# Routed tokens placed in a fixed area per expert, scattered batch by batch, with zeros written behind each expert's last token

## The chip, the cores and the metric

The kernel runs on one core of one Trainium2 chip. The core has a matrix engine (PE), a vector engine (DVE), a scalar engine (ACT), a general engine (POOL, also called GpSimd) and a queue engine (SP) that mostly issues DMAs. Each of them runs its own list of instructions in order, and they wait for one another only through semaphores. The metric is the time of one execution on the device in microseconds (us); lower is better.

## The reference

Two transformer decoder layers, width 128, on x of 4 batches x 512 tokens:

```python
x = x + L0_attn(layernorm(x))            # causal, 16 heads of 8
x = x + L0_xattn(layernorm(x), ctx)      # 77 context tokens
x = x + L0_ffn(layernorm(x))             # 8 experts, top 2
x = x + L1_attn(layernorm(x))
x = x + L1_xattn(layernorm(x), ctx)
x = x + L1_ffn(layernorm(x))             # ternary weights, conv over tokens
```

The change lies in L0_ffn:

```python
gate_logits = jnp.einsum('bsd,de->bse', x, gate_w) + gate_b
weights, indices = jax.lax.top_k(gate_logits, TOP_K)        # 2 of 8
weights = jax.nn.softmax(weights, axis=-1)
h = jnp.einsum('bsd,edh->ebsh', x, w1) + b1[:, None, None, :]
xh, gh = jnp.split(h, 2, axis=-1)
act = jax.nn.silu(gh) * xh                                  # 512 wide
out_e = jnp.einsum('ebsf,efd->ebsd', act, w2) + b2[:, None, None, :]
sel = jnp.take_along_axis(out_e, indices[..., None], axis=2)
return jnp.sum(sel * weights[..., None], axis=2)
```

## The kernel before

All 2048 tokens stay in SBUF as 16 tiles (NT) of 128 tokens, four per batch (QT = 4, NB = 4). The first stream of work is 32 attention units, numbered g: 0 to 15 for the causal self-attention (A0), 16 to 31 for cross-attention (X0), four units (of four heads) per batch. In unit g PE computes the scores of g, the probabilities-by-values products of g - 1 (`last_pv_pe`), the transposes of g - 2 (`finish_pe`), and, between the scores, the score maxima of unit g + 2, which DVE reduces (L605) out of three PSUM banks (`bank_turn`) that `take_bank` hands round; POOL turns the maxima into two bf16 parts, PE transposes them (`turn_pe`), DVE copies them and SP writes them into the stacked queries, with the loads of unit g + 3. `BESIDE` says which further task a unit carries: "merge" and "proj" of X0's batch b end its cross-attention and add it to x (`proj_dve`, L800). That happens for batches 0, 1 and 2 in units 24, 27 and 31 and for batch 3 in `end_pe` and `end_dve`.

Only after that begins the expert layer, in `moe_dve`, `moe_pe`, `moe_act`, `moe_pool` and `moe_sp`. For each batch: moments (`moments_dve`), reciprocal root on POOL (`norm_pool`, L475), normalise on DVE (L443) into `xn`, a copy of it to `xn_all` (ACT, L1712), transposes on PE (L522), a copy by ACT (L536), gate logits on PE (L1642, with the bias as a further matmul, L1643), and the choice of the top 2 on DVE (L1451 to L1471), which leaves one-hot rows `picked` and `routed`. When all four batches are done, PE ranks each token within its expert over all 16 tiles (16 matmuls, L1652 and L1654), and DVE rounds each expert's count up to tiles of 128 tokens, forms a running sum over the experts (`base`) and adds base x 128 to the rank: that is `place`, the row of a packed DRAM array `routed_tokens` of 40 tiles. Then POOL scatters, with 32 indirect DMAs (16 tiles x 2 choices, L1620). The rows that no token takes hold zeros that one DMA wrote over the whole array in unit 13 (L1139).

When all scatters have landed, SP loads tile after tile from `routed_tokens` (L1746), at most two ahead of PE, and the experts run over 39 tiles (`BUSY_TILES`): transpose (L1666), two 512-wide products with w1 (L1672), Silu on ACT, transposes (L1680), and the product with w2 (L1687). Which expert a tile belongs to comes from `tile_e`, a word that holds the experts of four tiles (`CODED`): PE and DVE each read it into a register and decode it for every fourth tile (`experts`). ACT stores each tile's output to `expert_outputs`. At the end POOL gathers each token's two rows with 32 more indirect DMAs (L1630) at the same `place_u`, and DVE adds them to x (L1595). `weights_dve` and `weights_pe` (L1877 to L1893) prepare the last layer's ternary weights; DVE does them behind the routing.

## Time and profile before

| | |
|---|---|
| median of 3 runs | 918.29 us (917.34 to 919.59) |
| profiled execution | 916.52 us, its span 914.80 us |
| busy in the span | PE 705.6 us (77%), DVE 576.9 (63%), ACT 407.0 (44%), POOL 291.7 (32%) |
| mean granted PE clock | 0.859 of full speed |
| DMA | 73.12 MB, 80 GB/s |

A profile is one execution. All times are measured from the start of the span. A row of the timeline is an instruction or a run of like ones: start, duration, engine, line, operation, output <- inputs, and in brackets how long the engine had sat idle and what ended it. The chain of waits is followed back from the last instruction, at each step to what released it.

### The profile page before, as it was taken

How to read it: one execution, taken by the hardware profiler on the slowest of the kernel's cores; microseconds unless marked ns; L12 is line 12 of the kernel's file. 1: busy time of each engine (PE TensorE's matmuls, PEld its weight loads, DVE VectorE, ACT ScalarE, POOL GpSimd, SP SyncE). 2: the span in 40 equal slices, each digit the busy share in tenths (PEclk: the TensorE clock that was granted, in tenths of full speed). 3: DMA queues.
4: the chain of work that ended last, by engine and by line, in shares of the span. 5: the costliest groups of instructions: out<-in, count | busy, mean ns of one | idle time of the engine just before them, and what ended most of it. 6: DMA issues, size and time to landing. Idle time of an engine off the chain costs nothing.

```text
span 914.8 us, 14449 instructions
## 1 busy us (share of the span) xinstructions
PE 705.6 (77%) x4718; PEld 344.0 (38%) x4718; DVE 576.9 (63%) x1493; ACT 407.0 (44%) x584; POOL 291.7 (32%) x535
## 2 busy tenths in 40 slices
PE   3489999989897865019999972468788888889787
PEld 1244454544344455005656541212222232323443
DVE  3767687766254455207777752676878888871564
ACT  1215566655545621003333321225566676676354
POOL 4634445556523111750000007621423123141220
PEclk9777999999658875559999995658999999999899
DMA  7623664656123130111111101620222211000000
GB/s 202 210 89 131 188 196 122 180 200 177 42 78 97 47 115 4 52 49 33 39 37 42 41 27 49 200 73 24 71 70 82 74 32 47 25 2 1 0 24 24
DMA packets 81627, 73.12 MB, mean 80 GB/s; under 512 B 14739, under 2 KB 74131, under 8 KB 81555
## 3 DMA queue, kind: packets, MB, share of 16 engines
q1 hardware_dynamic: 73458, 64.66, 22.7%
q0 software_dynamic: 2048, 4.20, 1.5%
q10 hardware_dynamic: 6048, 3.35, 1.2%
q8 instruction: 40, 0.66, 0.3%
q14 instruction: 33, 0.26, 0.1%
HBM read 41.85 MB, written 29.93 MB: 78 GB/s over the span
## 4 chain that ended last, share of the span: by engine, by line
PE 53%; DVE 21%; issue 9%; POOL 7%; DMA 5%; ACT 2%; SPq 1%; DVEq 0%; POOLq 0%; ACTq 0%
DVE mx L605 12%; PE bank_pv L728 9%; PE bank_turn L589 8%; PE bank_st L1929 4%; PE bank_turn L1672 4%; PE bank_st L1687 4%; PE bank_st L1672 3%; POOL routed_tokens L1620 3%; PE bank_st L693 3%; PE bank_st L1680 2%; PE bank_turn L747 2%; PE bank_turn L522 2%; DMA stk<-stack_kx 1%; DVE stats L424 1%; DVE xn L443 1%
## 5 line engine op out<-in xcount | busy, mean ns | idle before, releaser
L605 DVE TENSOR_REDUCE mx<-bank_turn 128x1 f32<-128x512 f32 (+3 forms) x512 | 297.2, 625 | 85.8 <-PE bank_turn L589 48.3
L708 ACT ACTIVATE probs<-bank_st 128x1024 f32<-128x1024 f32 (+4 forms) x288 | 245.6, 883 | 165.0 <-PE bank_st L693 163.5
L589 PE MATMUL bank_turn<-stk 64*128 64x512 bf16 (+4 forms) x768 | 187.1, 320 | 53.6 <-DVE mx L605 41.0
L693 PE MATMUL bank_st<-stk 64*128 64x512 bf16 (+4 forms) x576 | 181.4, 373 | 2.2 <-ACT probs L708 1.4
L728 PE MATMUL bank_pv<-probs,vsl 128*32 128x512 f32 (+4 forms) x1152 | 144.1, 574 | 5.2 <-POOL probs L716 4.1
L589 PEld LDWEIGHTS bank_turn<-stk 64*128 64x128 bf16 x768 | 59.9, 101 | 188.7 <-DVE mx L605 111.6
L1630 POOL DMA_INDIRECT w<-expert_outputs,place_u x32 | 30.9, 966 | 152.7 <-DMA expert_outputs<-probs 143.6
L522 PE MATMUL bank_turn<-ident,xn 128*128 128x128 f32 x80 | 19.4, 388 | 73.7 <-DVE xn L443 73.5
L716 POOL TENSOR_SCALAR_AFFINE_SELECT probs<-probs 128x256 f32<-128x256 f32 x128 | 51.8, 407 | 72.2 <-ACT probs L708 70.8
L617 POOL CAST neg<-mx 128x16 bf16<-128x16 f32 x48 | 9.4, 197 | 169.8 <-DVE mx L605 166.5
L1723 ACT COPY okT<-bank_st 128x512 f32<-128x512 f32 x39 | 22.8, 586 | 86.4 <-PE bank_st L1680 86.4
L693 PEld LDWEIGHTS bank_st<-stk 64*128 64x128 bf16 (+1 forms) x576 | 48.3, 97 | 16.8 <-ACT probs L708 8.1
L594 PE MATMUL bank_turn<-behind_even,even_q 64*128 64x128 bf16 x256 | 52.9, 228 | 0.0
L593 PE MATMUL bank_turn<-behind_pair,pair_q 64*128 64x128 bf16 x256 | 52.8, 228 | 0.0
L475 POOL TENSOR_TENSOR rstd<-var,mhalf 128x4 f32<-128x4 f32 x24 | 25.4, 1058 | 82.5 <-DVE var L430 82.4
L1719 ACT ACTIVATE probs<-probs 128x512 f32<-128x512 f32 x39 | 24.6, 631 | 51.7 <-DVE probs L1542 51.7
L1929 PE MATMUL bank_st<-f_w1c,w 128*128 128x512 f32 x96 | 47.3, 631 | 0.4 <-ACT w L531 0.4
L1687 PEld LDWEIGHTS bank_st<-w,okT 128*128 128x128 f32 x312 | 37.9, 191 | 25.0 <-issue 25.0
L1672 PE MATMUL bank_turn<-w,probs 128*128 x80 | 43.6, 631 | 3.6 <-issue 2.9
L536 ACT COPY xnT<-bank_turn 128x512 f32<-128x512 f32 x20 | 11.7, 585 | 74.8 <-PE bank_turn L522 74.8
L1687 PE MATMUL bank_st<-w,okT 128*128 x312 | 44.0, 284 | 0.8 <-ACT okT L1723 0.8
L522 PEld LDWEIGHTS bank_turn<-ident,xn 128*128 128x128 f32 x80 | 12.7, 194 | 80.4 <-DVE xn L443 59.4
(247 smaller groups left out, 1120.9 us busy)
## 6 DMA issues: line engine op xcount, KB each, us to landing
stk<-stack_A SPq DMA_DIRECT2D x64, 256.0 KB, 3.2
w<-in_M_w SPq DMA_DIRECT2D x12, 512.0 KB, 4.6
stack_A<-parts SPq DMA_DIRECT2D x15, 384.0 KB, 2.7
stack_A<-fill SPq DMA_DIRECT2D x8, 512.0 KB, 5.5
stk<-stack_X SPq DMA_DIRECT2D x16, 256.0 KB, 2.6
stack_A<-parts SPq DMA_DIRECT2D x15, 256.0 KB, 3.2
routed_tokens<-zero SPq DMA_DIRECT2D x1, 2560.0 KB, 11.4
probs<-routed_tokens SPq DMA_DIRECT2D x39, 64.0 KB, 1.8
```

The lines of the kernel that those rows point to most:

```text
L522: i = e.transpose(bank[:, j * P:(j + 1) * P], normal(ln)[:, j, :], ident[:])
L589: mm = e.matmul(o, stk[r, slot, 0, pp, qt * P:(qt + 1) * P], stk[r, slot, 1, pp, 0:keys], start=True, stop=not a.causal)
L593: e.matmul(o, half(pair_q, j), half(behind_pair, j), start=False, stop=False)
L594: mm = e.matmul(o, half(even_q, j), half(behind_even, j), start=False, stop=True)
L605: e.tensor_reduce(o.rearrange("p h q -> p q h"), bank_of((g, m))[:, 0:k * keys].rearrange("p (q h k) -> p q h k", q=len(tiles), h=len(hs)) ...
L693: mm = e.matmul(bank_st[j][0:a.kp, pp, 0:S - q0], stk[r, slot, 1, pp, kt * P:kt * P + a.kp], stk[r, slot, 0, pp, q0:S], start=True, stop=True)
L708: e.activation(probs[0:a.kp, probs_of(g, kt), j:HG:2, 0:n], bank_st[j][0:a.kp, :, 0:n], ACT.Exp, scale=1 / math.sqrt(HD)).then_inc(s["prob ...
L716: e.affine_select(out=o, in_=o, compare_op=ALU.is_ge, fill=0.0, base=0, pattern=[[0, 2], [1, P]], channel_multiplier=-1).then_inc(s["maske ...
L728: mm = e.matmul(bank_pv[VW * h:VW * (h + 1), q0:S], vsl[0:a.kp, slot, kt, h, :], probs[0:a.kp, probs_of(g, kt), h, 0:S - q0], start=(kt == ...
L1672: e.matmul(hid[t % 2][z], x_inT[:, t % 2], w1[:, bass.ds(ex[t], 1), z * FF:(z + 1) * FF].rearrange("p o n -> p (o n)"), start=True, stop=T ...
L1687: mm = e.matmul(y_bank[:, 0:D], actT[:, c * P:(c + 1) * P], w2[:, bass.ds(ex[t], 1), c, :].rearrange("p o n -> p (o n)"), start=(c == 0), ...
L1929: e.matmul(bank, f_xT[:, b, j * P + tap:j * P + tap + P], f_w1c[:, tap], start=(tap == 0), stop=False)
```

## The change

Each expert gets a fixed area of `REGION` = 32 tiles in `routed_tokens`, which so grows from 40 to 256 tiles. A token's row is then its rank in its expert plus the area's start (`regions`), and no longer depends on how many tokens the other experts have, nor on later batches. `place_dve` computes it for one batch; ranks carry over with `counted`, the number of tokens per expert so far. `ROUTE_PE`, `ROUTE_DVE` and `ROUTE_POOL` put the steps of batches 0 and 1 into units 24 to 31, and the rest stand in the `end_` functions. `scatter_pool` issues the eight scatters of one batch. The normalised tokens go straight into `xn_all`; the gate bias becomes an addition on DVE (`logits_dve`). The one DMA of zeros over the array becomes one of 64 KB for the last tile in unit 13 and eight of 64 KB in `moe_sp`, each at a row that SP reads into a register from the counts (`used`). The tiles to load are read from `tile_e` too (`blocks`): the word now holds 8 bits for each of three tiles (the block's number, of which the upper three bits are the expert). The outputs stay packed, so the gather has rows of its own, `place_y`. The 39 tiles and their work are the same.

```diff
+REGION = 2 * NT
+MT = 2 * NT + NE - 1
+CODED = 3
+BLOCK_BITS = 8
...
+ROUTE_PE = {28: [("turn", 0)], 29: [("gate", 0)], 30: [("rank", 0)]}
+ROUTE_DVE = {24: [("moments", 0)], 25: [("norm", 0)], 27: [("moments", 1)], 28: [("norm", 1)], 29: [("logits", 0), ("top", 0)],
+             30: [("place", 0)], 31: [("moments", 2)]}
+ROUTE_POOL = {25: 0, 28: 1}
...
-        scr_xn = nc.dram_tensor("routed_tokens", [MT * P, D], F32).ap()
+        scr_xn = nc.dram_tensor("routed_tokens", [NE * REGION * P, D], F32).ap()
...
         def unit_sp(e, g):
...
-                e.dma_start(scr_xn.rearrange("(t p) d -> p t d", p=P), zero[:].unsqueeze(1).to_broadcast([P, MT, D]))\
-                    .then_inc(s_zero, 16)
+                e.dma_start(scr_xn[(NE * REGION - 1) * P:NE * REGION * P, :], zero[:]).then_inc(s_zero, 16)
...
         def end_pe(e, g):
             last_pv_pe(e, g)
+            norm_pe(e, 2, 1)
+            finish_pe(e, g - 1)
             finish_pe(e, g)
+            gate_pe(e, 1)
             merge_pe(e, layer(g), NB - 1)
             for part in range(2):
                 proj_pe(e, layer(g), NB - 1, part)
+            rank_pe(e, 1)
+            for b in (2, 3):
+                norm_pe(e, 2, b)
+                gate_pe(e, b)
+                rank_pe(e, b)
+            count_pe(e)
+            weights_pe(e)
...
         def end_dve(e, g):
+            finish_dve(e, g - 1)
+            normalise(e, 2, 2)
             finish_dve(e, g)
+            logits_dve(e, 1)
+            top_dve(e, 1)
             proj_dve(e, layer(g), NB - 1)
+            moments_dve(e, 2, 3)
+            place_dve(e, 1)
+            logits_dve(e, 2)
+            top_dve(e, 2)
+            normalise(e, 2, 3)
+            place_dve(e, 2)
+            logits_dve(e, 3)
+            top_dve(e, 3)
+            place_dve(e, 3)
+            tiles_dve(e)
+            weights_dve(e)
+
+        def end_pool(e):
+            norm_pool(e, 2, 2)
+            scatter_pool(e, 0, 0)
+            scatter_pool(e, 0, 1)
+            norm_pool(e, 2, 3)
+            for b in (1, 2, 3):
+                for part in range(2):
+                    scatter_pool(e, b, part)
...
+        def rank_pe(e, b):
+            e.wait_ge(m["routed"], b + 1)
+            r = routed[:, QT * b:QT * (b + 1)].rearrange("p t n -> p (t n)")
+            o = take_bank(e, ("rank", b))
+            e.matmul(o[:, 0:QT * NE], before[:], r, start=True, stop=False, skip_group_check=True)
...
+        def place_dve(e, b):
+            tiles, n = slice(QT * b, QT * (b + 1)), 3 * b
+            e.wait_ge(*filled(("rank", b)))
+            e.tensor_tensor(place[:, tiles], bank_of(("rank", b))[:, 0:QT * NE].rearrange("p (t n) -> p t n", n=NE),
+                            regions[:].unsqueeze(1).to_broadcast([P, QT, NE]), ALU.add).then_inc(is_emptied(("rank", b)), 1)
...
+            e.tensor_copy(place_u[:, :, tiles], place_f[:, :, tiles]).then_inc(m["placed"], 1)
...
+        def scatter_pool(e, b, part):
+            if part == 0:
+                e.wait_ge(s_xn, norm_number(2, b) + 1)
+                e.wait_ge(m["placed"], b + 1)
+            for t in range(QT * b + 2 * part, QT * b + 2 * part + 2):
+                for k in range(2):
+                    e.indirect_dma_start(scr_xn, bass.IndirectOffsetOnAxis(ap=place_u[:, k, t:t + 1], axis=0),
+                                         xn_all[:, t, :], None).then_inc(m["scattered"], 16)
...
+        def blocks(e, t):
+            code = e.value_load(tile_e[0:1, bass.ds(t // CODED, 1)], min_val=0, max_val=2 ** (BLOCK_BITS * CODED) - 1)
+            return {t + n: (code >> (BLOCK_BITS * n)) & (NE * REGION - 1) for n in range(CODED)}
...
         def moe_sp(e):
...
+            e.wait_ge(m["used"], 1)
+            for n in range(NE):
+                behind = e.value_load(used[0:1, n:n + 1], min_val=0, max_val=NT * P)
+                e.dma_start(scr_xn[bass.ds(behind + n * REGION * P, P), :], zero[:]).then_inc(s_zero, 16)
+            e.wait_ge(s_zero, 16 * (NE + 1))
             e.wait_ge(m["scattered"], 16 * 2 * NT)
-            for t in range(BUSY_TILES):
+            e.wait_ge(m["tile_e"], CODED + 1)
+            at = {}
+            for t in range(MT):
+                if t not in at:
+                    at |= blocks(e, t)
                 if t > 1:
                     e.wait_ge(m["xT"], t - 1)
-                e.dma_start(x_in[:, t % 2], scr_xn[t * P:(t + 1) * P, :]).then_inc(m["tile_in"][t % 2], 16)
+                e.dma_start(x_in[:, t % 2], scr_xn[bass.ds(at[t] * P, P), :]).then_inc(m["tile_in"][t % 2], 16)
```

## Rows read from the trace of the kernel before

**Rows 1.** The page, part 4: shares of the chain of waits, by engine and line
```profile
PE 53%; DVE 21%; issue 9%; POOL 7%; DMA 5%; ACT 2%; SPq 1%; DVEq 0%; POOLq 0%; ACTq 0%
DVE mx L605 12%; PE bank_pv L728 9%; PE bank_turn L589 8%; PE bank_st L1929 4%; PE bank_turn L1672 4%; PE bank_st L1687 4%; PE bank_st L1672 3%; POOL routed_tokens L1620 3%; PE bank_st L693 3%; PE bank_st L1680 2%; PE bank_turn L747 2%; PE bank_turn L522 2%; DMA stk<-stack_kx 1%; DVE stats L424 1%; DVE xn L443 1%
```

**Rows 2.** Timeline, 347 to 408 us: start, duration, what [idle before <- what ended it]
```profile
362.39 0.18 DVE L1508 CAST place_u<-place_f 128x32 uint32<-128x32 f32 x1
...
363.44 1.25 POOL L1620 DMA_INDIRECT routed_tokens<-vraw,place_u  x1 [19.06 <-issue]
...
368.78 1.08 POOL L1620 DMA_INDIRECT routed_tokens<-vraw,place_u  x1 [0.30 <-issue]
...
402.99 0.95 POOL L1620 DMA_INDIRECT routed_tokens<-vraw,place_u  x1 [0.30 <-issue]
...
405.24 2.67 SPq L1746 DMA_DIRECT2D probs<-routed_tokens  x3
```

**Rows 3.** Timeline, 289 to 331 us: the last units of cross-attention
```profile
298.24 0.31 PE L589 MATMUL bank_turn<-stk 64*128 64x77 bf16 x2 [5.00 <-DMA stk<-stack_kx]
...
312.93 0.24 PE L589 MATMUL bank_turn<-stk 64*128 64x77 bf16 x2 [0.98 <-DMA stk<-stack_kx]
...
318.55 0.69 PE L693 MATMUL bank_st<-stk 64*77 64x512 bf16 x4
...
321.76 0.69 DVE L800 TENSOR_TENSOR x_sb<-x_sb,bank_turn 128x512 f32<-128x512 f32 x1 [0.31 <-PE bank_turn L789]
...
327.90 0.69 DVE L800 TENSOR_TENSOR x_sb<-x_sb,bank_turn 128x512 f32<-128x512 f32 x1 [2.85 <-PE bank_turn L789]
...
330.09 1.03 POOL L475 TENSOR_TENSOR rstd<-var,mhalf 128x4 f32<-128x4 f32 x1 [14.09 <-DVE var L430]
```

**Rows 4.** Timeline, 344 to 351 us: routing of batches 1 and 2 on VectorE
```profile
344.55 0.19 DVE L1451 COPY lg<-bank_turn 128x32 f32<-128x32 f32 x1 [1.26 <-PE bank_turn L1643]
...
346.40 0.19 DVE L1471 TENSOR_TENSOR routed<-picked 128x32 bf16<-128x32 f32 x1
...
350.53 0.19 DVE L1451 COPY lg<-bank_turn 128x32 f32<-128x32 f32 x1 [2.90 <-PE bank_turn L1643]
```

**Rows 5.** Groups of 328 to 364 us by shape: busy us, mean ns | idle before
```profile
L1642 PE MATMUL bank_turn<-gate_w,xnT 128*128 128x8 f32 x32 | 9.5, 372 | 2.7 <-ACT xnT L536 2.7
...
L443 DVE TENSOR_SCALAR xn<-x_sb,mv,rstd 128x128 f32<-128x128 f32 x16 | 4.5, 342 | 2.3 <-POOL rstd L475 2.3
```

**Rows 6.** Windows: length, busy us of each engine (x count), granted PE clock, DMA share
```profile
225.00:230.00 5.00, 2.89 (x36) 1.39 (x35) 1.42 (x4) 1.87 (x5) 4.88 (x9) 0.95 0.93 267
...
230.00:235.00 5.00, 5.00 (x37) 1.47 (x33) 1.17 (x3) 3.41 (x5) 3.02 (x9) 0.50 0.03 7
...
320.00:328.00 8.00, 5.82 (x44) 3.77 (x40) 2.43 (x8) 3.18 (x5) 0.00 (x0) 1.00 0.98 276
```

**Rows 7.** The chain of waits in order of time, experts: output matmuls of three tiles
```profile
419.49 0.96 PE bank_st L1687 x8
...
422.72 0.96 PE bank_st L1687 x8
...
426.50 0.96 PE bank_st L1687 x8
```

**Rows 8.** The tile loads' own line: ns min/median/max, first and last start
```profile
L1746 SPq DMA_DIRECT2D probs<-routed_tokens x39: 319/320/433, 405.2 to 530.1; - x39
```

**Rows 9.** Timeline: first and last of the feed-forward weights' work on VectorE
```profile
364.75 1.27 DVE L1877 TENSOR_REDUCE f_abs<-f_w 128x1 f32<-128x512 f32 x2
...
370.12 2.03 DVE L1893 TENSOR_TENSOR f_w1c<-f_taps,f_w 128x512 f32<-128x512 f32 x3
```

**Rows 10.** DMA issues by line: KB, median us from issue to landing
```profile
routed_tokens<-zero SPq DMA_DIRECT2D x1, 2560.0 KB, 11.4
probs<-routed_tokens SPq DMA_DIRECT2D x39, 64.0 KB, 1.8
```

**Rows 11.** The chain of waits in order of time, 195 to 330 us
```profile
225.60 3.12 POOL xn L443 x4
```

362 lines of the change are left out of this document (187 added, 175 removed).

## The prediction

> **What bounds the kernel now.** I read the page's chain of waits first, then the windows of the span, then the timeline of 290 to 410 us. The chain names PE for half of the span, and one POOL line, L1620, for 3% [rows 1]; the reader is to see that this is one solid block and not scattered pieces. The timeline shows it: `place_u` is ready at 362.57, the first scatter starts at 363.44, the 32nd at 402.99, and SP's first tile load at 405.24 [rows 2]. That is (402.99 - 363.44) / 31 = 1.28 us for each scatter, 41.8 us from the first scatter to the first load, and after 372.2, when DVE has finished the ternary weights [rows 9], no engine but POOL has anything to do. The spacing is the issue on POOL itself, 0.95 busy and 0.30 between two, not the landing. So the stage ends on POOL, and a scatter that starts earlier is worth its whole 1.28 us as long as POOL stays the last.
>
> Ahead of that block lies the routing, 330 to 362 us, a serial chain through DVE, POOL, PE and ACT in which POOL does only four roots of 1.0 us. One batch takes 350.53 - 344.55 = 5.98 us [rows 4].
>
> **The change part by part.**
>
> The block of scatters moves. After it POOL's list is: root of batch 2, 8 scatters (batch 0), root of batch 3, 24 scatters. The start S of the first scatter is set by the root of batch 2, which needs X0's projection of batch 2 (unit 31) and its moments. Before, the scores of unit 31 start at 318.55 and that projection's addition at 321.76 [rows 3]. What is put ahead of it:
> - Moments 0 and the normalising of batch 0 (units 24, 25; 1.5 and 1.1 us of DVE; 4.5 / 4 = 1.1 from [rows 5], 1.5 as between the end of L800 at 328.59 and the root at 330.09 [rows 3]) fall where PE sits 5.00 us for a load of unit 28 whose issue SP had queued behind a write of the stack [rows 3]. Cost 0; were the load not late, up to 2.6.
> - Moments 1 in unit 27: 1.5 us before the maxima of unit 28, against 0.98 that PE waits for a load at 312.93 [rows 3]: +0.5. The normalising of batch 1 in unit 28 (1.1, behind its root, 1.03, of which about 0.3 is hidden) stands ahead of the maxima of unit 29: +1.8.
> - The gate projection of batch 0 in unit 29 stands on PE ahead of unit 30's scores. Its 8 matmuls cost 9.5 / 32 = 0.30 each in a stretch at the half clock [rows 5], so 2.4, about 1.2 at full clock; ahead of it PE waits for ACT's copy, which stands behind two exponentials of unit 29, about 1.1: +2.3. The bias matmuls (as many again) are gone.
> - The ranks of batch 0 at the end of unit 30 wait for the top 2, 346.40 + 0.19 - 344.55 = 2.04 us on DVE [rows 4], mostly beside unit 30: +1.
> Queued behind these waits are PE's scores of units 30 and 31, and all the rest of cross-attention. Sum 5.6: unit 31 at 324.1, its projection 3.2 later at 327.3, then 0.7, moments 1.5, root 1.0 and 0.3: 330.8 at least. One of the three banks is held by batch 0's transposes while unit 29 makes its four maxima, and PE's clock may fall: in the trace it went from 0.95 to 0.50 after a stretch with PE busy 2.89 of 5 us, while 5.82 of 8 kept it at 1.00 [rows 6]. At the half clock, 1.2 GHz, the path of units 30 and 31 would be some 5 us longer. I take S = 332.5, between 330 and 336, nearer to the full clock since the new gaps are of 1 to 2 us.
>
> From S the list is 41.8 us as before, plus the root of batch 3 in the middle, 1.03 and 0.3 of handover, plus SP's read of the block word before the first load. No row shows a register read on SP; the nearest is on PE, where a tile that decodes takes (426.50 - 422.72) - (422.72 - 419.49) = 3.78 - 3.23 = 0.55 us more [rows 7]; I take 0.7, between 0.3 and 2. First load: 332.5 + 41.8 + 1.3 + 0.7 = 376.3 instead of 405.24: -28.9.
>
> What could be later than POOL: batch 3's root is at S + 8 x 1.26 + 1.0 = 343.6; one batch's chain is 5.98 before and shorter now by 8 bias matmuls; batch 3 is placed near 354, and its scatters' turn comes at 364: 10 us to spare. After it DVE has the tile table and the new gather rows, some 20 small operations of 0.17 to 0.5 us with their waits, 7.5 us, and the weights, 372.2 - 364.75 = 7.4 [rows 9]: done by 369, 7 us before the first tile. The eight zero DMAs wait for `used`, near 354.5; at 0.55 for the read and 0.32 for the issue [rows 7, 8] they take 7 us, then one landing, done by 364, 10 us to spare, and they fail to hide only above 2.2 us each. ACT's four copies of `xn` are gone, off the path.
>
> Experts: 39 tiles before and after. The decode comes every third tile: 13 times instead of 10, +3 x 0.55 = +1.65, between 1.0 and 2.2 since a word holds three tiles and not four. SP's reads hide: a load is issued after the transpose two tiles back and is needed two tiles, 6.5 us, later, and takes 0.32 to issue [rows 8] and 1.8 to land [rows 10].
>
> The large zero DMA, 2560 KB and 11.4 us from 218 us on [rows 10], is removed. Beside it the chain runs over POOL's normalising (3.12 us at 225.60, [rows 11]), not over a transfer: cost 0 either way, but the clock fell just there [rows 6], and another timing could save or add some microseconds: -5 to +2. The second stream gets its banks from a rotation that starts elsewhere: the same work, 0, within 1.5 either way.
>
> Sum: -28.9 + 1.65 = -27.3. Against the profiled execution, 916.52, that is 889.2; the median of the runs is 1.8 higher, so 918.29 - 27.3 = 891.0.
>
> A rule of the Trainium skill speaks against the overlap. What the rows show: the scatters at 363 to 372 ran beside DVE's work on the weights, and the longest but the first took 1.08 instead of 0.95 [rows 2]. The page "SBUF — State Buffer", section "SBUF: two separate sides", says that a VectorE operation in a mode that uses both port pairs locks GpSimd out, so that it can't write the descriptors of its own DMAs, and that such a DMA looks blocked by the VectorE operation. By that rule the scatters, which now stand beside DVE's routing, would stretch; by the trace hardly. What it would give is the second rival.
>
> **The rivals.**
> 1. The tail of attention is the victim: PE falls to 1.2 GHz in unit 29 or 30, and S is 336 to 338. For: the clock's fall after 225 us [rows 6]. Against: 320 to 328 stayed at full clock with more gaps than before it. Time 891.0 + 4.5 = 895.5.
> 2. Each scatter is held up by one small DVE operation: +0.2 for each of 32, +6.4: 897.4; at half a microsecond each, 907. For: the 1.08. Against: only one in seven of those beside DVE was longer.
> 3. Something else than POOL becomes last: the zeros, or batch 3's placing, and the stage ends at 380 to 388: 900. For: DVE's list is long and holds POOL's and PE's waits. Against: the 7 to 10 us to spare.
> 4. The early part gains from the missing zeros (clock or queue): 885.
> 5. It doesn't do what it says: the scatters of batch 0 wait in effect for the last placing, near 354 (by a wait or a queue that I overlook). First load at 354 + 41.8 + 0.7 = 396.5, -8.7 + 1.65: 911.
> 6. Slower than before: reading and decoding an address for every load makes SP the bound of the expert stage. A tile takes 3.23 to 3.78 us [rows 7]; the load hides until SP needs more than about 3.4 us for each. To turn the gain into a loss of 0.3% (2.8 us) the 39 tiles must lose 30 us, that is 0.77 each: SP at 4.15 us a load decides. At 4.5 it is 39 x 1.1 = +43, less 28.9: 933. For: nothing shows SP with registers. Against: PE reads the same kind of word in 0.55.
>
> **How the numbers follow.** The forecast, 886 to 897 with rival 1 left out, has 0.60. Rival 1 has 0.12, rival 2 0.10, rival 3 0.06, rival 4 0.05, rival 5 0.04, rival 6 0.03. The low end takes S = 330, a decode cost of 1.0 and some 3 us of rival 4: 883. The high end takes rivals 1 to 3 in, up to 903; outside are rivals 5 and 6 and the far ends of 2 and 4. About 0.3% is what a measurement of this kernel can tell from no change. Faster by more than that is all but rival 6 and a remnant of combinations: 0.96; within 0.3%: 0.015; slower 0.025.
>
> **What would show it right or wrong.** In the timeline of the changed kernel: the first scatter at 330 to 336; 32 scatters at 1.26 to 1.28 with one root among them; the first tile load at 374 to 380, directly behind the last scatter; no wait at the start of units 25 to 27 other than for DMAs; scores of unit 31 at 323 to 326 and the granted clock near 1.00 there; every third tile some 0.5 longer. It is wrong if POOL has gaps among the scatters (rivals 2, 3, 5), if SP's first load comes long after the last scatter, or if the tiles' period isn't 3.2 to 3.8.

## The result and the profile after

The changed kernel takes 908.31 us (median of 4 runs, 903.89 to 913.6), the kernel before 918.71 beside it (917.34 to 919.59); the ratio is 0.989, 95% interval 0.9841 to 0.994. The forecast was 891.0 with a range of 883 to 903: the sign was right, the gain is 10 us and not 27. In a second session (a session is a group of kernels run one after the other on one chip) the same kernel had 900.3 us over 6 runs against 915.98, ratio 0.9817, 0.9774 to 0.9861. One execution of `zeros_early2` (913.98 us) and one of the kernel before (1006.28 us) lie more than 1.5% above the fastest of their kernel and are left out of the medians and ratios below.

The profiled execution of after is the slowest of its four, 913.6 us with a span of 911.8. Its page, part 4, answers [rows 1]: the scatters are gone from the lines, PE and DVE have one point more each, and 1% (it was none) is waiting for something that the profile can't name.

```profile
PE 54%; DVE 22%; issue 10%; POOL 5%; DMA 4%; ACT 2%; SPq 1%; another core or an unknown queue 1%; DVEq 0%; POOLq 0%; ACTq 0%
DVE mx L583 12%; PE bank_pv L706 10%; PE bank_turn L567 8%; PE bank_st L2011 5%; PE bank_turn L1748 4%; PE bank_st L1748 4%; PE bank_st L1763 4%; PE bank_st L671 3%; PE bank_st L1756 2%; PE bank_turn L725 2%; PE bank_turn L519 2%; DVE stats L439 1%; DMA stk<-stack_A 1%; PE bank_turn L809 1%
```

The timeline of after, POOL from 340 to 385 us and then SP's queue from 376 to 398, answers [rows 2] and the last of [rows 3]:

```profile
340.38 1.01 POOL L472 TENSOR_TENSOR rstd<-var,mhalf 128x4 f32<-128x4 f32 x1 [15.82 <-DVE var L445]
341.58 1.30 POOL L1635 DMA_INDIRECT routed_tokens<-vraw,place_u  x1 [0.19 <-issue]
...
375.40 0.96 POOL L1635 DMA_INDIRECT routed_tokens<-vraw,place_u  x1 [2.39 <-DVE place_u L1554]
...
384.46 0.96 POOL L1635 DMA_INDIRECT routed_tokens<-vraw,place_u  x1 [0.30 <-issue]
```
```profile
377.72 14.35 SPq L1817 DMA_DIRECT2D routed_tokens<-zero  x8
394.13 3.08 SPq L1827 DMA_DIRECT2D probs<-routed_tokens  x3
```

Three things are off the forecast here: the first scatter is at 341.58 and not 332.5; the 25th scatter waits 2.39 us for its places; and the eight zeros, which were to be long done, are issued from 377.7 to 392.1, so that the first load comes 9.7 us behind the last scatter and not 2.25 as before.

The expert stage answers [rows 7]. The timeline of after, the output matmuls of four tiles: 3.24, then 4.02 for the tile with a decode, then 3.23.

```profile
405.40 1.12 PE L1763 MATMUL bank_st<-w,okT 128*128 x8
...
408.64 1.12 PE L1763 MATMUL bank_st<-w,okT 128*128 x8
...
412.66 1.12 PE L1763 MATMUL bank_st<-w,okT 128*128 x8
...
415.89 1.12 PE L1763 MATMUL bank_st<-w,okT 128*128 x8
```

**Milestones.** Each number is the start of an instruction in the timeline of one execution, in us: PE's first scores of units 26 and 31, first and last scatter (their starts), SP's first tile load, PE's first and last expert output, and the end of the span. "Slow steps" is explained under "What slows DVE and SP beside the scatters".

| kernel | unit 26 | unit 31 | first scatter | last | first load | first output | last output | span | slow steps |
|---|---|---|---|---|---|---|---|---|---|
| before | 298.35 | 318.55 | 363.44 | 402.99 | 405.24 | 416.10 | 544.14 | 914.8 | - |
| before_again | 298.56 | 319.29 | 364.19 | 404.26 | 406.50 | 417.52 | 545.04 | 915.6 | - |
| after | 300.56 | 334.04 | 341.58 | 384.46 | 394.13 | 405.40 | 537.36 | 911.8 | yes |
| repeat | 304.06 | 337.30 | 343.94 | 385.13 | 388.25 | 398.91 | 530.94 | 906.3 | no |
| repeat_look | 296.92 | 327.48 | 334.56 | 375.74 | 378.87 | 389.76 | 521.76 | 893.1 | no |
| after_look | 300.77 | 330.12 | 337.62 | 378.19 | 390.46 | 401.60 | 533.53 | 904.5 | yes |
| early_zeros | 301.63 | 335.10 | 342.74 | 383.96 | 387.37 | 398.33 | 530.35 | 902.9 | no |
| zeros_early2 | 302.22 | 333.13 | 342.36 | 384.17 | 388.49 | 404.38 | 536.14 | 908.3 | yes |
| routing_behind | 299.87 | 320.33 | 346.39 | 386.05 | 389.17 | 400.51 | 532.65 | 902.7 | no |
| late_pe | 297.65 | 323.76 | 337.45 | 378.08 | 388.49 | 399.57 | 531.47 | 904.5 | yes |
| filled_wait | 300.18 | 327.14 | 334.57 | 375.31 | 388.02 | 399.00 | 531.11 | 904.6 | yes |
| words4 | 299.55 | 328.87 | 336.27 | 376.88 | 389.54 | 400.39 | 528.43 | 899.4 | yes |
| words4_later | 298.19 | 329.09 | 346.19 | 387.00 | 390.11 | 401.35 | 530.11 | 901.0 | no |
| words4_landed | 302.26 | 333.37 | 342.60 | 385.91 | 389.01 | 400.10 | 528.81 | 901.5 | no |
| better | 308.81 | 336.29 | 343.89 | 385.15 | 388.55 | 399.57 | 525.24 | 900.5 | no |
| better2 | 301.76 | 329.68 | 336.80 | 377.33 | 389.37 | 400.47 | 525.97 | 899.7 | yes |
| better3 | 301.93 | 328.82 | 338.09 | 378.79 | 390.27 | 401.13 | 527.10 | 896.9 | yes |
| better4 | 295.55 | 323.34 | 330.17 | 371.38 | 379.93 | 395.09 | 521.08 | 896.1 | yes |

### The profile page after: what moved, and what is told of

Same layout as the page of the kernel before. It is cut to its first block, busy times and chain, and to the rows that moved or that the text cites. A ratio compares the mean times of both kernels' runs of the same rounds, so it can differ in the third digit from the quotient of the medians.

```text
span 911.8 us, 14699 instructions
## 1 busy us (share of the span) xinstructions
PE 711.0 (78%) x4684; PEld 339.6 (37%) x4689; DVE 580.5 (64%) x1523; ACT 406.3 (45%) x580; POOL 292.0 (32%) x536
## 4 chain that ended last, share of the span: by engine, by line
PE 54%; DVE 22%; issue 10%; POOL 5%; DMA 4%; ACT 2%; SPq 1%; another core or an unknown queue 1%; DVEq 0%; POOLq 0%; ACTq 0%
DVE mx L583 12%; PE bank_pv L706 10%; PE bank_turn L567 8%; PE bank_st L2011 5%; PE bank_turn L1748 4%; PE bank_st L1748 4%; PE bank_st L1763 4%; PE bank_st L671 3%; PE bank_st L1756 2%; PE bank_turn L725 2%; PE bank_turn L519 2%; DVE stats L439 1%; DMA stk<-stack_A 1%; PE bank_turn L809 1%
## 5 line engine op out<-in xcount | busy, mean ns | idle before, releaser
L567 PE MATMUL bank_turn<-stk 64*128 64x512 bf16 (+4 forms) x768 | 189.2, 324 | 52.8 <-DVE mx L583 44.4
L671 PE MATMUL bank_st<-stk 64*128 64x512 bf16 (+4 forms) x576 | 184.4, 380 | 2.2 <-ACT probs L686 1.4
L706 PE MATMUL bank_pv<-probs,vsl 128*32 128x512 f32 (+4 forms) x1152 | 149.9, 595 | 4.0 <-POOL probs L694 3.3
L1732 POOL DMA_INDIRECT w<-expert_outputs,place_y x32 | 30.9, 965 | 165.0 <-DMA expert_outputs<-probs 155.9
L519 PE MATMUL bank_turn<-ident,xn 128*128 128x128 f32 x64 | 14.6, 369 | 71.2 <-DVE xn L462 69.9
L1748 PE MATMUL bank_st<-w,probs 128*128 x76 | 40.5, 615 | 2.8 <-issue 2.8
L734 DVE RECIPROCAL rec<-bank_turn 128x16 f32<-128x16 f32 x48 | 12.2, 254 | 47.5 <-PE bank_turn L725 47.1
```

What stands on the lines that cost most here:

```text
L519: i = e.transpose(bank[:, j * P:(j + 1) * P], normal(ln, b)[:, j, :], ident[:])
L567: mm = e.matmul(o, stk[r, slot, 0, pp, qt * P:(qt + 1) * P], stk[r, slot, 1, pp, 0:keys], start=True, stop=not a.causal)
L671: mm = e.matmul(bank_st[j][0:a.kp, pp, 0:S - q0], stk[r, slot, 1, pp, kt * P:kt * P + a.kp], stk[r, slot, 0, pp, q0:S], start=True, stop=True)
L706: mm = e.matmul(bank_pv[VW * h:VW * (h + 1), q0:S], vsl[0:a.kp, slot, kt, h, :], probs[0:a.kp, probs_of(g, kt), h, 0:S - q0], start=(kt == ...
L1748: e.matmul(hid[t % 2][z], x_inT[:, t % 2], w1[:, bass.ds(ex[t], 1), z * FF:(z + 1) * FF].rearrange("p o n -> p (o n)"), start=True, stop=T ...
```

## The experiments

Theory A: the first scatter is late because the routing steps in the units of cross-attention drop PE's clock. Theory B: beside that, the eight zeros stand on the path, that is, SP would load the first tile earlier without them. The rivals: a chance of one execution; another cause of the clock's fall; and, for the zeros, that something else ends as late.

### The kernel again, and without the late zeros

> The changed kernel itself, once more, as the comparison for the kernels that ran beside it. Its earlier runs lie between 903.9 and 913.6, those of the kernel before within 2.3 us. If the spread belongs to the kernel and not to the chip, it shows again: 903 to 914 with the kernel before within 2 us of 918.5. In the trace I expect PE at half clock in a large part of 295 to 335 us again, the first scatter near 341, the first tile load near 394. If the half clock there was a chance of one execution, scores of unit 31 stand near 324 and the first scatter near 333, as I had forecast, and the time is near 900.

Measured: 900.3 us (897.91 to 907.99). The way from unit 26 to unit 31 is 33.2 us, as in after (33.5), so the late first scatter was no chance. But the zeros end before the last scatter, and the first load follows it by 3.1 us.

early_zeros: eight fixed blocks are zeroed in units 14 to 21 (they hold for these inputs alone).

```diff
+LAST_BLOCK = [1, 3, 7, 4, 3, 2, 4, 3]
...
+            if W_PIECES + 1 < g <= W_PIECES + 1 + NE:
+                n = g - W_PIECES - 2
+                last = n * REGION + LAST_BLOCK[n]
+                e.dma_start(scr_xn[last * P:(last + 1) * P, :], zero[:]).then_inc(s_zero, 16)
...
+            e.wait_ge(s_zero, 16 * (NE + 1))
             scatter_pool(e, 0, 0)
...
-            e.wait_ge(m["used"], 1)
-            for n in range(NE):
-                behind = e.value_load(used[0:1, n:n + 1], min_val=0, max_val=NT * P)
-                e.dma_start(scr_xn[bass.ds(behind + n * REGION * P, P), :], zero[:]).then_inc(s_zero, 16)
```

> The changed kernel, with the zeros behind each expert's last token taken off the end: eight zero blocks of 64 KB are written in units 14 to 21 at fixed places, over the block in which each area ends with these inputs, and the scatters wait for them; SP reads no count. (The fixed places hold for these inputs alone, so this is a measurement and not a version.) Theory 1, the zeros stand on the path: the last scatter starts at 384.5 as in the changed kernel, SP's first tile load follows 2 to 3 us behind it, near 387.5 and not 394.1, and the time is 6.5 us below that of the changed kernel. Theory 2, the zeros only fill a time in which SP would wait anyway, for the block words or for the scatters' landing: the first load stays within 2 us of 394 and the time within 1.5 us. A price for eight small writes in the attention units would show as unit 25 starting later than in the changed kernel; I expect none.

Measured: 903.21 us (898.37 to 905.97), ratio 0.9843 against 0.9817 for repeat. No gain; the first load is 3.4 us behind the last scatter. In executions like these two the zeros are hidden, as the forecast had it, and Theory B falls for them.

### Routing steps out of the units

routing_behind empties the three tables that put routing steps into units 24 to 31. The steps follow unit 31, in the `end_` functions (that part of the edit isn't shown), and the scatters start behind all four roots.

```diff
-ROUTE_PE = {28: [("turn", 0)], 29: [("gate", 0)], 30: [("rank", 0)]}
-ROUTE_DVE = {24: [("moments", 0)], ...}
-ROUTE_POOL = {25: 0, 28: 1}
+ROUTE_PE, ROUTE_DVE, ROUTE_POOL = {}, {}, {}
```

> The changed kernel, with every routing step of batches 0 and 1 moved out of the units of cross-attention to behind unit 31; the scatters still go batch by batch, now behind all four roots. Theory 1, the steps put into the units cost what they bring, since the waits on PE drop its clock: units 24 to 31 run as in the kernel before, scores of unit 31 near 318.5 to 320 with the granted clock near 1.00 from 305 to 325, and the first scatter at 336 to 340, earlier than the 341.6 of the changed kernel; the time is 2 to 5 us below it. Theory 2, the clock falls for another reason (the zero DMA that is gone, another phase): scores of unit 31 come near 334 again, the first scatter near 350, and the time is 5 to 9 us above the changed kernel.

Measured: 906.2 us (904.32 to 910.25), ratio 0.9895 (0.9849 to 0.9941), 6 us above repeat beside it, where I expected 2 to 5 us below. The wait ahead of unit 28 alone can't be what makes the units slow, for the clock falls there before the change too, to 0.52 from 295 to 305 us:

```profile
295.00:305.00 10.00, 6.76 (x47) 3.53 (x47) 2.77 (x8) 3.20 (x4) 0.56 (x3) 0.52 0.24 63
```

The windows behind it (length, busy us of each engine with its count, granted PE clock, DMA share and GB/s) of before, after and routing_behind, in this order:

```profile
305.00:315.00 10.00, 8.46 (x93) 4.26 (x92) 6.76 (x19) 6.23 (x8) 1.13 (x6) 1.00 0.25 64
315.00:325.00 10.00, 9.03 (x69) 4.43 (x65) 3.51 (x12) 6.93 (x10) 0.71 (x4) 1.00 0.50 131
```
```profile
305.00:315.00 10.00, 8.91 (x63) 5.02 (x61) 5.19 (x23) 4.33 (x5) 0.56 (x3) 0.64 0.13 33
315.00:325.00 10.00, 8.74 (x50) 3.18 (x50) 4.96 (x15) 3.73 (x5) 2.23 (x8) 0.53 0.12 32
325.00:335.00 10.00, 8.87 (x41) 5.13 (x41) 3.86 (x30) 4.16 (x6) 0.00 (x0) 0.50 0.01 2
```
```profile
305.00:315.00 10.00, 8.73 (x87) 4.61 (x86) 5.80 (x17) 5.58 (x7) 1.13 (x6) 0.88 0.27 64
315.00:325.00 10.00, 9.70 (x84) 4.43 (x79) 4.09 (x12) 7.77 (x11) 0.71 (x4) 1.00 0.28 88
```

With the steps behind the attention, units 26 to 31 take 20.5 us with the clock at 0.88 and 1.00, as in before (20.2, 20.7). With the steps in the units it is 29.4 to 33.5 in the four traces of the changed kernel, at 0.50 to 0.64 of the clock in after (0.50 is 1.2 GHz). So it is the routing steps. The clock does come back behind the wait for the load, and then falls a second time, as in repeat_look:

```profile
305.00:315.00 10.00, 8.17 (x68) 4.41 (x60) 6.29 (x28) 4.30 (x6) 2.09 (x7) 0.82 0.23 58
315.00:325.00 10.00, 8.36 (x43) 3.73 (x43) 4.11 (x27) 4.11 (x6) 0.71 (x4) 0.50 0.01 3
```

The intervals between the first scores of one unit and the next show where the time goes (us; the last three kernels belong to experiments below):

| kernel | 26 to 27 | 27 to 28 | 28 to 29 | 29 to 30 | 30 to 31 |
|---|---|---|---|---|---|
| before | 5.84 | 4.75 | 4.10 | 2.93 | 2.58 |
| routing_behind | 5.83 | 4.83 | 4.28 | 2.94 | 2.58 |
| after | 5.85 | 6.43 | 7.33 | 9.01 | 4.86 |
| repeat_look | 5.84 | 4.59 | 6.28 | 8.99 | 4.86 |
| late_pe | 5.84 | 4.36 | 5.38 | 5.76 | 4.77 |
| words4 | 5.84 | 4.35 | 6.42 | 7.85 | 4.86 |
| filled_wait | 3.84 | 4.22 | 6.19 | 7.85 | 4.86 |

The second half of my expectation for routing_behind fails: the first scatter is at 346.39, 26 us behind unit 31, and not at 336 to 340, since the serial chain then starts only there. From 315 to 325 us PE is as busy in after as in before (8.74 and 9.03 of 10 us) and gets less done, 50 matmuls against 69. The mix of matmuls isn't the same in the two; the durations of like ones, below, are the surer sign of half a clock.

late_pe leaves the moments, roots and normalising of DVE and POOL in the units and moves PE's steps, with the top 2 and the placing that follow them, behind unit 31 (the new order of the `end_` functions isn't shown):

```diff
-ROUTE_PE = {28: [("turn", 0)], 29: [("gate", 0)], 30: [("rank", 0)]}
-ROUTE_DVE = {24: [("moments", 0)], ...}
+ROUTE_PE = {}
+ROUTE_DVE = {24: [("moments", 0)], 25: [("norm", 0)], 27: [("moments", 1)], 28: [("norm", 1)], 31: [("moments", 2)]}
```

> The changed kernel with one half of the routing left in the units of cross-attention, that of DVE and POOL (moments, root and normalising of batches 0 and 1 in units 24 to 28, moments of batch 2 in unit 31). What PE has of it (transposes, gate projection and ranks of batch 0), with the top 2 and the placing that follow, goes behind unit 31. In the kernels before it, from the first scores of unit 26 behind the wait for a load to those of unit 31 took 20.2 us without routing steps (the kernel before), 20.5 with all of them behind (the last experiment), and 33.2 to 33.5 with all of them in. Theory 1, PE's own steps and their waits cost most of the 13: here it takes 21 to 25 us, with the granted clock at 1.00 from 310 to 325, and the first scatter comes at 334 to 340. Theory 2, the DVE operations ahead of the maxima cost most: 28 to 32 us, the clock at 0.50 in the larger part of 310 to 330, the first scatter at 342 to 346. Time by theory 1: 3 to 8 us below the changed kernel; by theory 2: within 2 us of it or above.

Measured: 907.35 us (903.78 to 910.96), ratio 0.9858. Units 26 to 31 take 26.1 us: between the theories. The steps that are left cost 6 (26.1 against 20.2), those that were moved the other 3 to 7. The clock goes with theory 2, 0.50 from 315 to 325 although PE's own steps are gone. The last interval shows it best: 4.77 us without the ranks, 4.86 with them, 2.58 in before, so it is the clock and not the ranks. The first scatter is then 13.7 us behind unit 31 instead of 7. The changed kernel itself wasn't run beside it, so its time can't be compared with that kernel's.

What PE's part costs is seen in the timeline of after, PE in units 29 to 31:

```profile
321.90 0.24 PE L567 MATMUL bank_turn<-stk 64*128 64x77 bf16 x1 [0.66 <-DVE mx L583]
...
322.91 1.93 PE L706 MATMUL bank_pv<-probs,vsl 77*32 77x512 f32 x8
326.13 1.09 PE L725 MATMUL bank_turn<-ident,oT 128*128 128x128 f32 x4 [1.28 <-ACT xnT L533]
...
327.37 1.88 PE L1493 MATMUL bank_turn<-gate_w,xnT 128*128 128x8 f32 x8
329.18 1.08 PE L671 MATMUL bank_st<-stk 64*77 64x512 bf16 x4
...
334.04 1.08 PE L671 MATMUL bank_st<-stk 64*77 64x512 bf16 x4
```

From the scores of unit 29 (320.17) to those of unit 30 (329.18) it is 9.0 us against 2.9 in before: 1.28 for ACT's copy, 1.88 for the gate projection, and the eight matmuls of L706 take 1.93, where in before (L728, clock at 1.00) they take 1.06 to 1.07.

filled_wait puts 14 matmuls, whose result is overwritten, ahead of PE's wait for the load of unit 28.

```diff
+            if m == 0 and g in FILLED:
+                bank = take_bank(e, (g, m))
+                for _ in range(FILLED[g]):
+                    e.matmul(bank[:, 0:P], ident[:], ident[:], start=True, stop=True)
             if m == 0:
                 e.wait_ge(s["slot"][slot], 16 * SLOT_DMAS * (g // UNITS + 1))
-            bank = take_bank(e, (g, m))
+            if not (m == 0 and g in FILLED):
+                bank = take_bank(e, (g, m))
```

> The changed kernel with 14 matmuls of 128x128 (identity times identity, overwritten by the ones that follow) put on PE ahead of its wait for the load of unit 28, where it stood idle for 2.6 to 4.1 us and where the granted clock fell from 1.00 to 0.50. It asks whether that wait is what the clock never came back from. Theory 1, the wait starts the fall: the clock stays at 1.00 through 295 to 310, the intervals between scores of units 26, 27 and 28 fall from 5.8 and 6.4 to about 4.5, and with PE in the full clock the routing steps cost what they take by themselves: from the scores of unit 26 to those of unit 31 26 to 28 us, not 33.4. Theory 2, the waits that the routing steps bring drop the clock themselves: it is at 1.00 until about 312, then at 0.50 again from 317 to 333, and it takes 29 to 32 us. Time 5 to 7 us below the changed kernel by theory 1, 0 to 4 below by theory 2.

Measured: 903.93 us (903.11 to 906.37), ratio 0.9813. Units 26 to 31 take 27.0 us. The window of filled_wait that holds units 27 and 28:

```profile
300.00:310.00 10.00, 8.80 (x96) 4.70 (x94) 6.65 (x25) 6.38 (x8) 1.13 (x6) 1.00 0.16 37
```

The clock stays at 1.00 there; later it falls again (0.67 for 315 to 325). Both theories hold in part: the wait for the load brings one fall, and the routing's waits a second one. The five kernels with the filled wait (filled_wait and the four called better) take 26.9 to 27.9 us, the eleven traces with all the routing in the units and no filling 29.3 to 33.5. Within one session the difference is 1.4 to 3.6 us. The sure part of it is the first interval, 3.84 us instead of 5.84, and that one is just as long in before. So the filling takes away a loss that the kernel before has too. Behind unit 28 hardly anything changes: from there to unit 31 it is 18.9 us against 19.1 in words4, of the same session, and 9.6 in before. The cost of the routing steps is in those three intervals. Nobody tried the filling on the kernel before.

### What slows DVE and SP beside the scatters

scatters_held holds POOL until the gather rows and the zeros are done.

```diff
             norm_pool(e, 2, 2)
-            scatter_pool(e, 0, 0)
-            scatter_pool(e, 0, 1)
             norm_pool(e, 2, 3)
-            for b in (1, 2, 3):
+            e.wait_ge(m["gathered"], 5)
+            e.wait_ge(s_zero, 16 * (NE + 1))
+            for b in range(NB):
```

> The changed kernel, with all 32 scatters held back until the gather rows are done and the eight zeros have landed. It asks what slowed DVE's chain (358 to 387 us) and SP's zeros (0.7 us for a register instruction, 14.35 us for eight) in the changed kernel. Theory 1, the scatters in flight slow the sequencers of the other engines: without them DVE goes from the logits of batch 3 to the gather rows with no stall above 0.7 us, some 12 to 15 us instead of 22.2 (364.1 to 386.4), and the eight zeros take under 9 us. Theory 2, the stalls belong to this code or these engines (first execution of the code, the latency of the semaphores): DVE shows stalls of 1.8 to 5.8 us at the same lines, and the zeros take 12 to 15 us again. The scatters then start near 375 to 385 and the time is some 25 to 35 us above the changed kernel, either way.

Measured: 929.55 us, no stalls, zeros in 8.35 us. It told nothing yet, since repeat and early_zeros had no stalls either, with the scatters in flight. late_pe, words4 and filled_wait, of the next session, all had them. Here is what they look like: DVE in after_look, then the same lines in repeat_look.

```profile
372.52 0.48 DVE L1587 TENSOR_TENSOR tile_le<-moe_cum,iota_t 128x312 f32<-128x312 f32 x1 [2.55 <-remote]
...
376.02 0.48 DVE L1594 TENSOR_REDUCE tile_f<-tile_jump 128x39 f32<-128x312 f32 x1 [2.31 <-remote]
377.42 0.20 DVE L1596 TENSOR_TENSOR tile_f<-tile_f,iota_t 128x39 f32<-128x39 f32 x1 [0.92 <-DVE tile_f L1594]
```
```profile
357.40 0.53 DVE L1587 TENSOR_TENSOR tile_le<-moe_cum,iota_t 128x312 f32<-128x312 f32 x1
...
358.48 0.48 DVE L1594 TENSOR_REDUCE tile_f<-tile_jump 128x39 f32<-128x312 f32 x1
359.00 0.20 DVE L1596 TENSOR_TENSOR tile_f<-tile_f,iota_t 128x39 f32<-128x39 f32 x1
```

The instructions are about as long as ever, but behind the one of L1594 the next starts 1.40 us after it and not 0.52. I call these slow steps. DVE waits for its own last result or for nothing named, from some 13 to 19 us after the first scatter until a few us after the last; SP issues the zeros at the same crawl (14.4 to 28.5 us for eight instead of 8.2 to 8.5), while POOL's scatters keep their 1.26 us.

words4_later holds the first scatter until batch 1 is placed, words4_landed makes POOL wait for all earlier scatters ahead of each batch; both are built on words4 (under "The decodes"):

```diff
             norm_pool(e, 2, 2)
+            e.wait_ge(m["placed"], 2)
             scatter_pool(e, 0, 0)
```
```diff
             for b in (1, 2, 3):
+                e.wait_ge(m["scattered"], 16 * 8 * b)
```

> The kernel with words of four tiles, with the first scatter held back until batch 1 is placed (some 7 us). Between the traces so far there is a split. In after, late_pe, words4 and filled_wait, whose first scatter starts at 334.6 to 341.6 us, DVE and SP take 0.7 or 1.4 us for each step from some 13 to 17 us after the first scatter until a few us after the last, the zeros come behind the scatters, and the first tile load is at 388.0 to 394.1 however early the scatters began. In repeat, early_zeros, routing_behind and scatters_held, with the first scatter at 342.7 to 369.5, nothing of this is seen. Theory 1, an early first scatter brings the slow steps on: here, with the first scatter at 342 to 344, there are none, the eight zeros take 8.3 us, and the first load follows 3.1 us after the last scatter, near 389. Theory 2, it is a matter of the execution: the slow steps may be there or not, whatever the start. The time is that of words4 within 2 us either way.

> The kernel with words of four tiles, where POOL waits ahead of each batch of scatters until all earlier ones have landed (some 2.3 us each for batches 2 and 3, nothing for batch 1, behind the root). Theory 1, the slow steps of DVE and SP come from scatters that pile up in their queue: with never more than 8 of them on the way there are none, the zeros are out before the last scatter, and the first load comes 3.1 us after the last scatter, near 336 + 39.6 + 1.3 + 4.6 + 3.1 = 384.6, 4 to 5 us earlier than in words4. Theory 2, any scatters in flight will do: the steps are slow all the same, and the first load is at 388 to 392.

> The changed kernel once more, for its trace. By the theory that an early first scatter brings the slow steps on, they are there if the first scatter starts before 342 us, and absent if it starts after 342.7; by the theory that it is a matter of the execution, there is no such border. The way from the scores of unit 26 to those of unit 31 should be 33.2 to 33.9 us again, and that from the first to the last output of the experts 132.0.

Measured: 902.79, 903.26 and 894.88 us, one run each, and no slow steps in any of the three. repeat_look is the unchanged changed kernel, and its first scatter is the earliest of that kernel, 334.56: the border at 342 us that I had read out of eight traces falls, and with it the test of the queue, for there was nothing left for words4_landed to cure. It is also the execution that comes nearest to the forecast. Its timeline:

```profile
334.56 1.30 POOL L1635 DMA_INDIRECT routed_tokens<-vraw,place_u  x1 [0.19 <-issue]
...
375.74 0.96 POOL L1635 DMA_INDIRECT routed_tokens<-vraw,place_u  x1 [0.30 <-issue]
```
```profile
357.54 8.31 SPq L1817 DMA_DIRECT2D routed_tokens<-zero  x8
378.87 4.66 SPq L1827 DMA_DIRECT2D probs<-routed_tokens  x4
```

Then two kernels on one chip, one after the other, the changed one and the one with the scatters held:

> The changed kernel once more, beside the one with all scatters held back, on the same chip. The slow steps of DVE and SP were there in after and in all three traces of changed kernels of one call (late_pe, words4, filled_wait), and in none of the eight of two other calls; in the same traces, and in before_again, the landings of the scatters are missing from the list of DMA issues, and elsewhere they are there (2.2 to 2.3 us). So they may belong to the chip. Theory: if the landings are missing here, the slow steps are there and the zeros come behind the scatters; if the landings are listed, they are absent and the zeros take 8.3 us.

> The changed kernel with all scatters behind the gather rows and the zeros, once more, on the chip of the look before. If that one shows slow steps and this one shows none until the scatters start, it is the scatters in flight that slow the other sequencers on such a chip; if both show them, it is something else in the code; if neither does, nothing is told.

Measured: 906.31 us with slow steps, and 933.83 us without. SP's queue in held_again:

```profile
360.55 8.49 SPq L1817 DMA_DIRECT2D routed_tokens<-zero  x8
```

So where slow steps occur, they need the scatters in flight; this rests on one pair of executions. Every trace with scatters beside the routing had them in four sessions (after; late_pe, words4, filled_wait; after_look, better2, better3; zeros_early2, better4), and none in the other two (repeat, early_zeros, routing_behind; words4_later, words4_landed, repeat_look, better). Among these kernels it is the session that decides. What it is about the session is open, and the chip alone isn't it: the two sessions of repeat and of late_pe ran on the same chip, one without slow steps and one with them. The DMA issues (KB, us from issue to landing) give one more sign, here of after_look and then held_again:

```profile
routed_tokens<-vraw,place_u POOLq DMA_INDIRECT x32
```
```profile
routed_tokens<-vraw,place_u POOLq DMA_INDIRECT x32, 2.3
```

The scatters' landings are missing in all nine traces with slow steps and in before_again, and listed in all others. The Trainium skill, page "NOTIFIC — the notification-queue block", section "7.1 Overflow: three behaviours, one of which stalls the engine", says that the path that takes the records of a trace can hold up the engines that produce them. Lost records and slowed sequencers in the same traces may belong together in that way, though the page has losing and stalling as two settings of one queue. No run here shows it: in before_again DVE was done 9 us after the first scatter, too early for slow steps, and whether an execution that isn't recorded has them at all stays open.

zeros_early2 is early_zeros once more, better4 is better3 with four of the zeros read and issued by ACT and four by SP (`zeros_behind` holds the loop over the areas):

```diff
+        def moe_act(e):
+            e.wait_ge(m["used"], 1)
+            zeros_behind(e, range(NE // 2, NE))
```

> The kernel of early_zeros once more (eight zero blocks written in units 14 to 21, at places that hold for these inputs alone). Its first trace had no slow steps, and there the zeros of the changed kernel were hidden, so nothing could be gained. If this chip shows slow steps (by the landings missing from the DMA list), the first load should come at the later of two times: 3.1 us behind the last scatter, or some 3 us behind DVE's last word of the block table, which stood at 382.1 to 382.3 in after and after_look. That is 384 to 386, against 390.5 and 394.1 there, so the zeros by themselves cost 4 to 9 us on such a chip. If there are no slow steps, the first load is 3.1 to 3.5 us behind the last scatter, as before.

> As better3, with four of the eight zeros read and issued by ACT and four by SP. Where steps are slow, SP needed 15.3 us from the count to the last of eight zeros in the changed kernel; with two engines, each pays for four, and the first load should come 4 to 5 us earlier than in better3 if both are slowed alike by the scatters and not by each other: 385 to 386, and 893 to 895. Where steps are not slow, the zeros were hidden already and nothing changes. If the reads of the two engines get in each other's way, it comes at 388 to 390.

Measured: 906.39 us (898.32 to 910.14, three executions), ratio 0.9835 (0.9713 to 0.9957), and 899.38 us (897.87 to 900.52), ratio 0.9807 (0.9721 to 0.9893), both with slow steps. I had expected 893 to 895 for better4. Without the zeros the first load is only 4.3 us behind the last scatter, and yet the first output comes 20.2 us behind it, as in after (20.9). DVE in zeros_early2 shows why, and after_look how near to it the zeros were:

```profile
394.35 1.90 DVE L1977 TENSOR_TENSOR f_w1c<-f_taps,f_w 128x512 f32<-128x512 f32 x3
396.16 0.28 DVE L1648 COPY probs<-bank_turn 128x128 f32<-128x128 f32 x1
```
```profile
389.84 1.89 DVE L1975 TENSOR_TENSOR f_w1c<-f_taps,f_w 128x512 f32<-128x512 f32 x3
393.03 0.29 DVE L1642 COPY probs<-bank_turn 128x128 f32<-128x128 f32 x1 [1.29 <-PE bank_turn L1742]
```

The first tile's copy stands on DVE behind the table, the gather rows and the ternary weights, and under slow steps this list ends 0 to 2.4 us before PE has the first tile ready (DVE's idle time ahead of that copy: 1.89 in after, 2.36 in late_pe, 1.29 in after_look, 0.92 in filled_wait, 0.4 and 0.5 in better2 and better3, none in words4). Take the zeros away, or split them as better4 does (first load 8.6 us behind the last scatter, first output 23.7), and DVE's list is last. The price of the zeros by themselves is thus 0 to 2.4 us there and nothing elsewhere, and not the 4 to 9 us that I expected; that of the slow steps, first output against last scatter, is 20.2 to 23.7 instead of 13.8 to 14.5, some 6 to 10 us.

### The decodes

words4 gives PE and DVE words of their own, four tiles of 3 bits in each; SP keeps its blocks. How DVE makes the new words isn't shown.

```diff
-            code = e.value_load(tile_e[0:1, bass.ds(t // CODED, 1)], min_val=0, max_val=2 ** (BLOCK_BITS * CODED) - 1)
-            return {t + n: (code >> (BLOCK_BITS * n + 5)) & (NE - 1) for n in range(CODED)}
+            code = e.value_load(tile_x[0:1, bass.ds(t // WORD, 1)], min_val=0, max_val=NE ** WORD - 1)
+            return {t + n: (code >> (3 * n)) & (NE - 1) for n in range(WORD)}
```

> The changed kernel, where PE and DVE read the expert of a tile from a word of their own, with four tiles of 3 bits each as in the kernel before; SP still reads the block from its word of three tiles. In the changed kernel a tile without a decode takes 3.23 us and one with a decode 4.00 (12 of them behind the first), before 3.79 (9 of them). Theory 1, the cost is that of PE's and DVE's decodes and their number: tiles with a decode fall back to about 3.8, there are 9 of them, and from the first to the last output takes 128.0 us again and not 132.0. Theory 2, SP's reads and its computed addresses add to it: every third tile still shows some 0.2 to 0.5 more, and the stage takes 129.5 to 132. The time is 4 us below the changed kernel by theory 1, 0 to 2 by theory 2.

Measured: 903.56 us (901.09 to 904.2), ratio 0.9815. From the first to the last output 128.04 us; the nine tiles with a decode take 3.80 on average. In the changed kernel it is 131.9 to 132.0 in all four traces, twelve tiles with 3.99; before, 128.04 and 127.52, nine tiles with 3.81 and 3.73. So a decode costs 0.76 in the changed kernel and 0.58 in before (0.49 in its second trace), and there are three more of them: 12 x 0.76 - 9 x 0.58 = 3.9. words4_later and words4_landed, with the words of words4 in another session, have 128.76 and 128.71, so a decode of the same word costs 0.56 to 0.68, and all that SP's reads can add is 0.7 of the 4 us. How much of the higher price is the width of the fields isn't shown. The 4 us are seen in this stage alone; in the time of the whole kernel (ratio 0.9815, repeat 0.9817) they are not.

### Versions that keep what the experiments showed

> The kernel before, once more, for its trace: so far one execution of it stands against several of the changed kernel. In that one the scores of unit 26 start at 298.35 and the stage from the last expert output to the end takes 370.7 us; in five executions of changed kernels 298.8 to 304.1, and 370.0 to 375.4. If the early part and the second stream only vary from execution to execution, this one lies inside those bounds, away from the first; if it is the change that lengthens them, it lies within 0.5 us of the first.

Measured: 917.35 us; unit 26 starts at 298.56, the second stream takes 370.6 us, within 0.3 of before. The changed kernels have 369.8 to 375.4 and unit 26 at 295.6 to 304.1 (the kernel better apart). So these parts vary in the traces of the changed kernels, mostly to the worse. Two traces are few to call the kernel before steady: its executions spread by 9 to 13 us within each session (911.41 to 923.92 in that of repeat). Why these parts vary, I did not find out.

> A version with three edits of the changed kernel: the zeros are written early and for any counts (16 blocks of each expert's area, 1 MB for each, one area in each of units 14 to 21), PE and DVE read the experts from words of eight tiles, and 14 matmuls fill PE's wait ahead of unit 28. From the experiments: 12 decodes of 0.77 become 4 of 0.5 to 0.8, so -6 to -7 us from the first to the last output (125 to 126); the filled wait takes 4 to 6 us off the units 26 to 31; the first scatter at 335 to 338, and the first load 3.1 us behind the last scatter, at 378 to 382, if nothing but the zeros stood behind the scatters. That gives 885 to 892. The rival: DVE's table of tiles is itself late by its slow steps (it ended at 381.9 in words4), so the first load is at 382 to 386 and the time 890 to 896. The early zeros are 8 MB beside the loads of the self-attention units; if they get in the way, unit 26 starts later than 304, and the time rises by as much.

Measured: 902.28 us (893.53 to 906.61), ratio 0.9784. I had expected 885 to 892. The words gave what they should (125.67 us), and unit 26 starts at 308.81, later than in any other trace (at most 304.1), as the expectation had it if the 8 MB of zeros got in the way.

> The changed kernel with two edits: words of eight tiles for the experts that PE and DVE read, and the 14 matmuls that fill PE's wait ahead of unit 28; the zeros as in the changed kernel. From the first to the last output of the experts 125.7 us as measured, 6.3 less than in the changed kernel; from the scores of unit 26 to those of unit 31 27 us, 3 to 6 less. Together 9 to 12 below the changed kernel: 889 to 893 where the scatters end last, and some 4 more where the zeros come behind them. The rival: what the filled wait gains is given back in the routing, which ends the same place by its own chain; then it is 6 to 7 below, 894 to 897.

> As better2, with the normalising of batches 0 and 1 done by POOL and not by DVE, where it stood ahead of the maxima of units 27 and 30 and PE waited 1.25 us for them. If these waits keep the clock down, the scores of unit 31 come 22 to 25 us after those of unit 26, not 27, and the first scatter and the time are 2 to 4 us below better2; if not, 26 to 27 us and within 1 us of it. POOL has 1 to 3 us of work in 15 there, and one normalising takes it 3.1 us; if its negations of the maxima come late by that, unit 31 comes later instead.

better3 against better2:

```diff
-ROUTE_DVE = {24: [("moments", 0)], 25: [("norm", 0)], 27: [("moments", 1)], 28: [("norm", 1)], 29: [("logits", 0), ("top", 0)],
+ROUTE_DVE = {24: [("moments", 0)], 27: [("moments", 1)], 29: [("logits", 0), ("top", 0)],
...
                     norm_pool(e, 2, ROUTE_POOL[g])
+                    normalise(e, 2, ROUTE_POOL[g])
```

Measured: 898.44 us (895.77 to 901.74), ratio 0.9776 (0.9734 to 0.9818), and 897.03 us (891.36 to 900.95), ratio 0.9755 (0.9706 to 0.9805). The first is above both of its forecasts (889 to 893, some 4 more with late zeros; the rival 894 to 897). The two can't be told apart by time. Units 26 to 31 took 27.9 and 26.9 us, so DVE's normalising ahead of the maxima was worth 1 us at most and not 4. The first load stood at 389.4 and 390.3 in both, by the slow steps. Both beat the kernel before by 20 us and the changed kernel of their session (906.31, one run) by 8 to 9.

## Why the prediction was off, point by point

**The step that failed** is the first sum of the prediction, "Sum 5.6" for the routing steps that are put ahead of unit 31, with "nearer to the full clock since the new gaps are of 1 to 2 us". Measured, units 26 to 31 took 9.2 to 13.3 us longer than before, at half the clock for the most part. A second one failed beside it in after: "10 us to spare" for the zeros and for batch 3, where first scatter to first load took 8.8 us more than forecast. The block of scatters itself moved as foreseen.

The forecast in milestones, on the span of the profiled execution (887.5; 1.7 us between span and time and 1.8 from there to the median make 891.0), against the four traces of the changed kernel (after, repeat, repeat_look, after_look):

| stretch | forecast | measured |
|---|---|---|
| scores of unit 26 at | 298.35 | 300.6, 304.1, 296.9, 300.8 |
| unit 26 to unit 31 | 25.8 | 33.5, 33.2, 30.6, 29.4 |
| unit 31 to first scatter | 8.4 | 7.5, 6.6, 7.1, 7.5 |
| first scatter to first load | 43.8 | 52.6, 44.3, 44.3, 52.8 |
| first load to first output | 10.9 | 11.3, 10.7, 10.9, 11.1 |
| first to last output | 129.7 | 132.0, 132.0, 132.0, 131.9 |
| last output to the end | 370.7 | 374.4, 375.4, 371.3, 371.0 |
| span | 887.5 | 911.8, 906.3, 893.1, 904.5 |

In after the miss of 24.3 us is 7.7 for the routing steps, 8.8 for the slow steps between scatters and load, 3.7 in the second stream, 2.3 for the decodes and 2.2 ahead of unit 26; the other rows give -0.5.

- **The sum of 5.6 us for the routing steps in the units** is 9 to 13 us. Its parts were counted at the full clock and one after the other. By intervals, forecast against the four traces: 27 to 28 is longer than before by -0.3 to 2.2 (forecast 0.5), 28 to 29 by 2.2 to 3.2 (forecast 1.8), 29 to 30 by 4.9 to 6.1 (forecast 2.3), 30 to 31 by 2.3 (forecast 1.0), and this last is the clock, as late_pe shows. The trace of before had the sign: PE's long wait ahead of unit 28 ends at 298.24 [rows 3], the clock is 0.52 from 295 to 305 and 1.00 from 305 to 315. The prediction looked at the fall after 225 us alone. With the routing's waits behind it, the clock came back for a few microseconds at most and fell again. Rival 1 named this and gave it 0.12 and 4.5 us; it is the normal case, and its size is 4 to 8 us over the forecast.
- **"Cost 0" for the steps of units 24 and 25** holds: the wait for the load of unit 28 shrinks with them, from 5.00 to 2.58 us in after. That wait still costs 2.0 us of clock in the interval behind it, as filled_wait shows, before the change and after it.
- **Unit 31 to the first scatter** and **the 41.8 us of scatters with one root and one read between them** were right: 44.3 us in both traces without slow steps, forecast 43.8. The 0.7 for SP's read of the word was near: the load follows the last scatter by 3.1, before by 2.25, so 0.9.
- **"Done by 364, 10 us to spare" for the zeros, "done by 369" for DVE, "batch 3 is placed near 354"**: where steps are not slow they are late by the attention's delay at most, and hidden (repeat_look: last zero issued at 365.9, DVE done at 369.5, last scatter at 375.7). Where they are slow, the margins of 7 to 10 us go, and rival 3 is true, at 8.3 to 8.5 us (52.6 and 52.8 against 44.3). In after batch 3's placing holds up the 25th scatter by 2.1 us, and the zeros hold up the load. The margins came from rows of an execution in which DVE was done 9 us after the first scatter and no other sequencer but POOL's had work beside them, which could not show this.
- **Rival 2**, DVE stretching each scatter, is false. Nearly all scatters of all traces take 0.95 to 0.96 us with 0.30 between two. The longest behind the first of a series, 1.48 us, stands beside DVE's work on the weights (repeat_look, at 367.63, with one of 1.08 ahead of it; the same in repeat, early_zeros and before_again), and the two together cost some 0.7 us and not 6. The Trainium skill, page "SBUF — State Buffer", section "SBUF: two separate sides", has GpSimd locked out while VectorE runs an operation in a mode that uses both port pairs. No run here shows which of these operations do, so the "would stretch" of the prediction went further than the page. What happened is the reverse: the others were slow beside the scatters.
- **The decodes**: the number was right (three more), the price of one was not. I took 0.55 from one tile of [rows 7], with a word of four fields of 3 bits; with three fields of 8 bits it is 0.76. The term is 3.9 to 4.0 and not 1.65, and outside its own bounds of 1.0 to 2.2.
- **The second stream, 0 within 1.5**: 0.3 to 4.7 us longer in four traces of the changed kernel, against 0.1 between two of the kernel before. **The removal of the large zero DMA**, or whatever else moves the early part: -1.4 to +5.7 at unit 26, not the gain that rival 4 had. Both are the width that the range lacked. Its low end is also added up wrong: 891.0 less 2.5 (S = 330), 0.65 (decodes) and 3 is 884.9 and not 883.
- **Rivals 5 and 6** are false: the scatters start with batch 0's places, and tiles without a decode stay at 3.23 us, so SP never bounds the experts.

That one trace, repeat_look, comes within 5.6 us of the forecast span is luck in part: its unit 26 starts 1.4 us early, and it has no slow steps.

## What to carry to other kernels

Work that is put into the waits of a loop that PE bounds can cost more than its own time, if its waits bring PE's clock down: price it, and the loop around it, at half the clock too. Filling a long wait of PE is worth a try of its own, whatever else is changed. When a long serial chain is laid beside a long series of DMAs, a margin read from a trace in which the two never overlapped is no margin. A value that every tile decodes is worth a word of its own, with as many tiles in it as fit: the number of decodes (12, 9 or 4) did more than the price of one (0.49 to 0.77 us).

## What was not expected of the hardware

- Beside indirect DMAs in flight, the steps of DVE and SP came at 0.70 or 1.40 us each in four sessions of six (a zero DMA with its read and address: 1.0 us each without, 1.8 to 3.6 with), from some 13 to 19 us after the first scatter on. In the other two sessions, with the same scatters, nothing of it.
- 14 matmuls of 128x128 whose result nobody reads made the interval behind them 2.0 us shorter (3.84 instead of 5.84), by the granted clock (1.00 from 300 to 310 us; 0.50 in after).
- The same kernel, in executions that differ in nothing, started unit 26 anywhere from 296.9 to 304.1 us, with a granted clock that fell and rose at other places. In the only two traces of the kernel before it was 298.35 and 298.56.
